# Layer 2's attention in units of one key head, the first batch's run within layer 1's steps and its split weights kept in DRAM for the second

## What is computed

```python
x = layernorm(x + attn(x, Wq, Wk, Wv, Wo))   # layer 1: 16 heads of 128, a token sees 5 blocks of 64
# layer 2, for each batch b:
scores = x[b] @ w_router                     # one score a token
idx = sort(top_k(scores, 128))               # the 128 best tokens, in order
sel = x[b, idx]                              # batch 0's and batch 1's: S = 256 rows
h = rms_norm(sel, ln1_w)
q, kk, v = h @ wq + bq, h @ wk + bk, h @ wv + bv   # 16 query heads, 8 key and value heads
q, kk = rope(q, pos), rope(kk, pos)
att = softmax(causal(q @ kk.T / sqrt(128)))  # causal over all 256 rows: batch 1 also sees batch 0
x1 = sel + (att @ v) @ wo
mlp = (silu(h2 @ w_gate) * (h2 @ w_up)) @ w_down   # h2 = rms_norm(x1, ln2_w)
out = layernorm(x + scatter(x, idx, gate * (x1 + mlp) + (1 - gate) * sel))
```

## Time and profile before

| | |
|---|---|
| median of 3 runs | 1433.35 us (1432.47 to 1434.08) |
| profiled execution, its own time | 1435.52 us |
| its span, first to last instruction | 1433.5 us |
| mean granted TensorE clock | 0.953 |
| busy: PE, DVE, ACT, POOL | 1286.4, 905.2, 606.8, 313.4 us |

### The profile page before, as it was taken

How to read it: one execution, slowest core, us unless ns; L and a number is a source line. 1 busy time by engine, 2 the same in 40 slices (tenths; PEclk the granted TensorE clock), 3 DMA queues, 4 the chain that set the end, 5 groups by cost and what they waited for, 6 DMA issues and landing times.

```text
span 1433.5 us, 19759 instructions
## 1 busy us (share of the span) xinstructions
PE 1286.4 (90%) x7624; PEld 1145.9 (80%) x7624; DVE 905.2 (63%) x2328; ACT 606.8 (42%) x1388; POOL 313.4 (22%) x221
## 2 busy tenths in 40 slices
PE   6999999999999999999999999999998733767795
PEld 5898989889898988877879898989886633666795
DVE  4556565665565565787866556565556787686465
ACT  4444444444444444333434444444444222435352
POOL 2101120202020111231211021111202462252374
PEclk9999999999999999999999999999998876798798
DMA  5100110101010110133101010101100443253262
GB/s 172 35 22 30 31 44 30 45 16 45 15 45 30 45 65 10 64 99 118 45 26 45 15 45 26 34 30 40 40 33 1 161 147 96 77 170 124 75 207 101
DMA packets 70846, 89.61 MB, mean 63 GB/s; under 512 B 3360, under 2 KB 52512, under 8 KB 70752
## 3 DMA queue, kind: packets, MB, share of 16 engines
q1 hardware_dynamic: 70336, 87.04, 18.7%
q0 software_dynamic: 416, 1.31, 0.3%
HBM read 79.43 MB, written 8.91 MB: 62 GB/s over the span
## 4 chain that ended last, share of the span: by engine, by line
PE 67%; DVE 21%; ACT 7%; issue 3%; DMA 1%; POOL 0%; SPq 0%; ACTq 0%; DVEq 0%; POOLq 0%
PE proj L759 33%; PE y L759 10%; PE s L759 9%; PE o L759 8%; DVE arena L1179 8%; ACT arena L1020 4%; PE tp L831 4%; ACT prob L1054 2%; DVE prob L1214 2%; DVE work L1296 2%; DVE work L1388 1%; DVE yacc L1248 1%; ACT prob L1126 1%; DVE bn_out L1261 1%; DVE work L1391 1%
## 5 line engine op out<-in xcount | busy, mean ns | idle before, releaser
L759 PE MATMUL proj<-arena 128*128 128x256 f32 (+1 forms) x3552 | 649.3, 334 | 11.7 <-DVE arena L1179 7.5
L759 PEld LDWEIGHTS proj<-arena 128*128 128x128 f32 x3552 | 547.6, 192 | 74.1 <-DVE arena L1179 9.6
L1509 POOL TENSOR_TENSOR arena<-wraw,arena 128x1024 fp32r<-128x1024 f32 x98 | 242.8, 2487 | 936.0 <-ACT arena L1020 936.0
L1054 ACT ACTIVATE prob<-prob,stat 128x384 f32<-128x384 f32 (+1 forms) x256 | 151.0, 590 | 499.6 <-DVE stat L1214 499.6
L1179 DVE TENSOR_TENSOR arena<-proj,arena 128x512 fp32r<-128x512 f32 (+1 forms) x282 | 159.1, 569 | 314.1 <-ACT arena L1020 312.8
L759 PE MATMUL o<-arena 128*128 128x256 f32 (+1 forms) x1248 | 255.1, 333 | 8.8 <-DVE arena L1179 5.8
L759 PE MATMUL s<-arena 128*128 128x384 f32 (+3 forms) x1008 | 224.4, 340 | 10.8 <-DVE arena L1179 10.8
L759 PE MATMUL y<-arena 128*128 128x512 f32 (+1 forms) x888 | 214.7, 379 | 8.4 <-DVE stat L1419 4.4
L759 PEld LDWEIGHTS s<-arena 128*128 128x128 f32 x1008 | 175.2, 195 | 30.8 <-DVE arena L1179 15.7
L759 PEld LDWEIGHTS o<-arena 128*128 128x128 f32 x1248 | 185.8, 199 | 15.0 <-DVE arena L1179 7.7
L1179 DVE TENSOR_TENSOR arena<-tp,arena 128x384 fp32r<-128x384 f32 (+2 forms) x273 | 142.4, 522 | 83.5 <-ACT arena L1020 83.0
(11 more groups left out here) (136 smaller groups left out, 565.2 us busy)
## 6 DMA issues: line engine op xcount, KB each, us to landing
wraw<-in_L_attn_Wq SPq DMA_DIRECT2D x16, 512.0 KB, 3.3
wraw<-in_L_attn_Wk SPq DMA_DIRECT2D x16, 512.0 KB, 3.3
wraw<-in_L_attn_Wv SPq DMA_DIRECT2D x16, 512.0 KB, 3.3
wraw<-in_L_attn_Wo SPq DMA_DIRECT2D x16, 512.0 KB, 3.7
wraw<-in_L_ffn_wq SPq DMA_DIRECT2D x16, 512.0 KB, 5.1
yacc<-in_L_attn_hidden_states SPq DMA_DIRECT2D x16, 256.0 KB, 3.0
y_dram<-yacc SPq DMA_DIRECT2D x16, 256.0 KB, 3.2
out<-work SPq DMA_DIRECT2D x16, 256.0 KB, 2.1
```

What stands on the lines that cost most here:

```text
L759: ins = e.matmul(out_ap, l[a], r[b], start=first and i == 0 and j == 0, stop=final and i == n - 1 and j == 2, skip_group_check=skip)
L1054: e.activation(prob[s][:, 0:n], prob[s][:, 0:n], ACT.Exp, bias=stat[:, 4 * s + 1:4 * s + 2], scale=-1.0, accum_out=stat[:, 4 * s + 2:4 * s ...
L1509: e.tensor_tensor(lo, wraw[n % RAW_SLOTS][:], hi.bitcast(F32), ALU.subtract).then_inc(*G_.inc("wsplit", n, "lo"))
```

## The change

Layer 2's attention is cut anew. A **unit** is one key head n with its two query heads: `u1` the product of 512 columns (256 of q, 128 of k, 128 of v) with one piece of `wq` (uA) and one of k and v side by side (uB), its bias and v's split; `ur` the rotation; `u2` the transposes of q and k and their split; `u3` the scores, maximum and exponential; `un` the division; `u4` the transposes of the probabilities; `u5` the product with v; `u6` the product with 256 rows of `wo` (uC). Each is one stage of a generator.

- **Batch 0's** eight units run in groups 11 to 14 of layer 1, two a group, started at r = 2 and r = 9. All PSUM of a unit is one bank: `proj1` for the first, `y` for the second. The gather's follow-up (`routed_in(0)`) moves in front of them. Layer 1's output projection moves by a step, to r = 3 to 10.
- The three split pieces of each unit are written to DRAM (1 MB each, hi and lo, `wsave`), and batch 0's k and v too (`ukeep`). **Batch 1's** units read them back (`wback`, `ukback`) and split nothing. Behind step 255 ten slots take such pieces instead of five.
- Room: `O_SLOTS` falls from 3 to 2, and the transposed probabilities lie in a ring of 5 blocks instead of 8; where a tile's blocks wrap, its split is done in two instructions.
- Behind step 255 only layer 1's end, the choice of batch 1's tokens, and then batch 1's eight units stand, one started at each step. The units share one buffer of probabilities, `uprob`.

```diff
-O_SLOTS = 3
+O_SLOTS = 2
...
+PT_BLOCKS = 5
...
+UNIT_GROUPS = range(NG + 3, NG + 7)
...
+        for G in range(NB * NG):
+            b, g = divmod(G, NG)
+            pieces = dict(q=Wq, v=Wv, k=Wk)
+            stream += [((which, b, g), columns(pieces[which], g)) for which in ("qvk" if G > 0 else "qkv")]
+            if G - 1 in UNIT_GROUPS:
+                stream.append(unit_pieces(2 * UNIT_GROUPS.index(G - 1) + 1)[2])
+            if G >= 1:
+                stream.append((("o", *divmod(G - 1, NG)), rows(Wo, (G - 1) % NG)))
+            if G in UNIT_GROUPS:
+                n = 2 * UNIT_GROUPS.index(G)
+                stream += [*unit_pieces(n), *unit_pieces(n + 1)[:2]]
...
+        for n in range(NKV):
+            stream += [((which, 1, n), None) for which in ("uA", "uB", "uC")]
...
+                if is_kept(n):
+                    saved[slot_of[n]].plan(n)
+                    job("wsave", n)
...
+        def unit(b, n, banks):
             bs = n % 2
+            hold(f"work{bs}", ("ubias", b, n), V_, "ur", b, n, "vlo")
+            job("ubias", b, n)
+            yield
+            need("uA", b, n)
+            need("uB", b, n)
...
+            hold(to["u1"], ("u1", b, n), V_, "u1", b, n, "bias")
+            job("u1", b, n)
+            for which in ("uA", "uB"):
+                retire((which, b, n), "u1", b, n, "made")
+            yield
...
+            job("ur", b, n)
+            yield
...
+            job("u2", b, n)
...
+                job("ukeep", n)
+            yield
...
+            hold("uprob", ("u3", b, n), T_, "u4", b, n, "made")
+            job("u3", b, n)
+            if b == 1 and n + 2 < NKV:
+                bring_back(n + 2)
+            yield
+            job("un", b, n)
+            yield
...
+            job("u4", b, n)
+            yield
...
+            job("u5", b, n)
+            yield
+            need("uC", b, n)
...
+            job(kind, b, n)
+            retire(("uC", b, n), kind, b, n, "made")
...
-            if 4 <= r < 12 and 1 <= G and u < END:
-                project_out(G - 1, r - 4)
+            if 3 <= r < 11 and 1 <= G and u < END:
+                project_out(G - 1, r - 3)
...
-            if u == END - 3:
-                running.append(routed_in(0))
...
-            if u - END in FIRST_STEPS:
-                running.append(project2(0, FIRST_STEPS.index(u - END)))
+            if G in UNIT_GROUPS and r in (2, 9):
+                n = 2 * UNIT_GROUPS.index(G) + (r == 9)
+                running.append(unit(0, n, ["proj1" if r == 2 else "y"] * 6))
+            if u == END - 4:
+                add_slots(XT_SLOTS, "qk", NHEADS - 1, "q", 1, "made")
+            if u == END + 3:
+                add_slots([PT_SLOT], "pv", NHEADS - 1, TT - 1, "made")
...
-        for n in range(len(FIRST_STEPS), len(QKV_ORDER)):
-            step(project2(0, n))
         while len(selected) < NB:
-            step(attend2(0, next(pairs)))
-        step(routed_in(1), attend2(0, next(pairs)))
-        step(attend2(0, next(pairs)))
+            step()
+        step(routed_in(1))
...
-        for k in range(17):
...
+        for k in range(NKV):
+            step(unit(1, k, [f"proj{k % 2}", "s0", "s1", "tp", "y", "o0"]))
...
                 elif kind == "o":
                     H, half = key
                     if H >= O_SLOTS:
-                        act.wait_ge(*T_.at("out", (H - O_SLOTS) // HG, TT - 1, "made"))
+                        act.wait_ge(*T_.at("out", (H - O_SLOTS) // HG, 4 * half + 3, "made"))
...
+                    if tenant[n] is not None and is_kept(tenant[n]):
+                        act.wait_ge(*saved[slot_of[n]].at(tenant[n]))
...
+                elif kind == "wsave":
...
+                    sp.wait_ge(*(G_ if split_on[n] == "G" else V_).at("wsplit", n, "lo"))
+                    e.dma_start(w_dram[3 * m + "ABC".index(which[1])].bitcast(F32), whole[slot_of[n]].bitcast(F32)
+                                ).then_inc(saved[slot_of[n]].sem, 16)
...
+                elif kind == "wback":
...
+                    sp.wait_ge(*saved[slot_of[source]].at(source))
+                    e.dma_start(whole[slot_of[n]].bitcast(F32), w_dram[3 * m + "ABC".index(which[1])].bitcast(F32)
+                                ).then_inc(back_loaded[slot_of[n]].sem, 16)
```

More of the change, by code:

```diff
@@ L453, in build @@
         selected = []
-        rope_taken = []
         def choose(b):
@@ L498, in choose @@
             job("find", b)
-            job("gather", b, *rope_taken)
+            job("gather", b)
             selected.append(b)
+            if not tail:
+                yield
+                yield from routed_in(b)
         h_there = []
@@ L559, in attend2 @@
             yield
[L560 to L569 removed]
+            hold(to["u5"], ("u5", b, n), V_, "u5", b, n, "lo")
+            job("u5", b, n)
+            yield
+            need("uC", b, n)
@@ L571, in residual2, with bring_back @@
+            if b == 0 or n == 0:
+                hold(to["u6"], ("u6", b, n), V_, "u6", b, n if b == 0 else NKV - 1, "sum")
+            kind = "u6" if b == 0 or n == NKV - 1 else "u6part"
+            job(kind, b, n)
+            retire(("uC", b, n), kind, b, n, "made")
+        def bring_back(n):
+            for what in ("k", "v"):
+                kv_back[n % 2].plan(n, what)
+            job("ukback", n)
         def residual2(b):
-            hold(f"work{4 + b}", ("res", b), V_, "fin", b, "row")
@@ new lines, in tensor_program @@
+                    ins.then_inc(*T_.inc("u1", b, n, "made"))
+                elif kind == "u2":
+                    b, n = key
+                    dst = bank[bank_of["u2", b, n]]
+                    pe.wait_ge(*freed(bank_of["u2", b, n], "u2", b, n))
+                    pe.wait_ge(*V_.at("ur", b, n, "sum"))
+                    for k in range(3):
+                        ins = e.transpose(dst[:, k * P:(k + 1) * P], work[4 + n % 2][:, k * P:(k + 1) * P], ident[:])
+                    ins.then_inc(*T_.inc("u2", b, n, "made"))
+                elif kind == "u3":
```

610 lines of the change are left out of this document (317 added, 293 removed).

## The result

The changed kernel takes 1505.8 us (median of 4 runs, 1504.1 to 1507.3) against 1432.9 for the kernel before (4 runs, 1431.9 to 1434.1): ratio 1.0508, 95% interval 1.049 to 1.0526, slower by 73 us. Forecast were 1447 us and a range up to 1470. The direction was right and the size was not. The profiled span is 1505.5 us.

A forecast was written before the change was run, and what follows sets the result against it. TensorE was taken to bound layer 1, and waits the 329 us tail behind step 255. Terms 45 + 41 - 8 - 28 - 37 + 1 - 0.5 gave +13.5 on 1433.5: 1447 us, range 1412 to 1470.

The forecast's parts named there:

- A: Layer 1: TensorE's work for batch 0's eight units, 5.6 us each, costs its full duration, +45 us.
- B: Layer 1's unit groups: TensorE waits for weight splits at r = 4 and r = 12, plus clock and VectorE load, +41 us.
- `O_SLOTS` = 2: Layer 1, r = 10: ScalarE waits 1.4 us for the last output tile; put at nothing, 1 us a group if uncovered.
- The ring: Layer 1: extra instructions for wrapping blocks, 0.25 us in 2 steps of 5; nothing, 1 us a group if uncovered.
- C: End of layer 1's steps: the double split of batch 0's first pieces goes, with its waits, -8 us.
- D: Last output projection and layer norm: without project2, 32 us instead of 60.0, -28 us.
- E: Choice of batch 1's tokens: other work standing in its chain goes, 33 us left of 69.7, -37 us.
- F: Batch 1's units: rounds of 10.3 us through the single `uprob` buffer, then shorter ones; 105 us against 104.6, +1.
- G: Residual, MLP and end: same instructions with one addition less, -0.5 us on 94.9 us.
- Rival 1: Splits hidden in layer 1 and VectorE's reordering free: 1402 us, halfway 1422; chance 0.27 with the halfway case.
- Rival 2: Batch 1's units: returning 1 MB weight pieces bind the rounds at 12.5 us, +15, so 1462 us; chance 0.13.
- rival 3: Layer 1: splits wait for 1 MB saves to land, holding up ScalarE's exponentials, +40, so 1487 us; chance 0.08.

The follow-up runs named there:

- experiment 13: Changed kernel with late output-tile copies, two probability buffers, earlier load of batch 0's norm weights, no weight splits for batch 0's units: 1398.4 us, 0.9757 of the kernel before.
- experiment 8: Changed kernel, but batch 0's units use the group's split Wq piece, without own loads, splits and saves: 1453.7 us, 1.0142 of the kernel before.
- Experiment 6: Changed kernel with low parts of all weight pieces on VectorE instead of GpSimd in the groups with units: 1489.8 us, 1.0401 of the kernel before.
- Experiment 1: Kernel before with two output tiles used instead of three and the output projection one step earlier: 1460.8 us, ratio 1.0202.
- experiment 4: Kernel before, three output tiles kept, with only the output projection one step earlier (r = 3 to 10): 1440.6 us, ratio 1.0049.
- experiment 5: Changed kernel with output-tile copies two steps later and the projection back at r = 4 to 11: 1483.0 us, 1.0342 of the kernel before.
- experiment 2: Kernel before with only the ring of five blocks and its split copies, three output tiles kept: 1435.3 us, ratio 1.0026.
- experiments 10 and 11: Changed kernel with late copies, VectorE low parts, second probability buffer, batch 0's rows normed five steps later: 1454.0 us; then norm weights loaded at the gather: 1450.7 us.
- Experiment 9: Changed kernel with a second buffer for the probabilities of batch 1's odd units: 1483.0 us, 1.0333 of the kernel before.
- experiment 7: Changed kernel saving only unit 0's three pieces (3 saves of 1 MB, not 24), reused by all batch 1 units: 1500.6 us, 1.0485 of the kernel before.
- experiment 14: Kernel before with one edit, output-tile halves copied two steps later: 1421.0 us, ratio 0.9926.

## Why the prediction was too low

**A (+45): right.** Two units cost 12.7 us a group in experiment 13 (against a plain group of 65.8) and 11.6 in experiment 8 (79.4 against 67.8); 11.2 were forecast. At 12 us, four groups are 48.

**B (+41): the waits I named were right; the division that GpSimd holds up was left out, and the clock behind the waits was mis-sized.** At r = 4 TensorE waited 2.1 us in group 13 (forecast 2.2), at r = 12 3.7 and 0.6 (forecast 3.8 and 1.9): 26.0 us in four groups, forecast 32. Not in the sum was the division held up by GpSimd: 12.2 us in four groups. I had weighed it in the sentences on the Trainium skill (SBUF — State Buffer, "Who interferes with whom") and left it out. The trace agrees with that page here, also where it says that a VectorE instruction with both inputs in SBUF contends: the low part of v took 2.48 us, while one that reads one input from PSUM (line 1302) took its usual 0.55 in the same 5.04 us. Experiment 6 shows that GpSimd's low parts cause it: without them the wait falls to 3.4 us. And the clock: I took 5 us for all four groups. TensorE was busy 329.7 us in the four groups, and 310.3 with the same work at full clock in experiment 13, so the lower clock cost some 19. The stretches of 7.5 and 3.4 us shown behind the two long waits of a group ran at 0.58 and 0.57. 26 + 12 + 19 + 48 = 105, measured 102.8; the forecast had 86.

**`O_SLOTS` = 2 at nothing: wrong, and in every group.** The text said "ScalarE waits at r = 10 for the last output tile, 1.4 us, with one exponential behind it that TensorE needs a step later: nothing". The wait came as named, 1.25 us. The cover failed: behind the exponential also stands the step's split of k or q, which the scores of r = 12 need, and the row of the projection that would have filled r = 11 had moved to r = 10. "1 us a group if that cover fails" was in the text too, but not in the sum or the range. Experiment 1 gives 29 us for it together with the projection's earlier place, 7 of them for the place (experiment 4); experiment 5 takes 23 back.

**The ring at nothing:** 4 us (experiment 2).

**The rows of batch 0 in group 10:** not in the prediction at all. Group 10 grew by 8.7 us, of which 3.6 come with the two output tiles (73.6 us in experiment 1). For the rest there is the wait of 3.8 us for the norm. It is one of order on VectorE and not of the gather, which fits that later steps didn't cure it (experiments 10 and 11). The mean clock of that group was 0.93.

**C (-8): not seen.** The last 15 steps took 60.6 us instead of 59.6. With nothing else to fill them, each of the last three transposes waited 1.1 to 1.3 us for its division.

**D (-28): -25.4. E (-37): -40.1.** The two chains were forecast at 32 and 33 us and measured 34.6 and 29.6; that their sum came right to 1 us is partly luck.

**F (+1): the mechanism right, the later rounds wrong.** Experiment 9 shows that the single buffer sets the rounds, since without it the seven together fell from 76.4 to 53.3 us. The first u4 came after 28 us (forecast 29), and the first three rounds, forecast at 10.3 us, took 9.8, 11.2 and 12.4. But I had made those behind them shorter, 7 us each, because u1 falls out of them; they took 10.6, 14.4, 9.6 and 8.4. Without u1, TensorE waited for VectorE instead. In the one of 14.4 the rotation's addition and v's low part on VectorE took 2.64 and 2.43 us beside GpSimd's low parts for the MLP. +6.5 in all.

**G (-0.5):** +1.1.

**The rivals.** Rival 1 (splits hidden) is what experiments 8 and 13 build by leaving the splits out: its gain is real, its condition isn't met. Rival 2 (returning weights bind) falls for the changed kernel with experiment 9, where the same weights come back in rounds of 7.6 us on average instead of 10.9, rival 3 (saves block ScalarE) with experiment 7. The 59 us by which the forecast was low are: 17.4 in the groups 1 to 9, where nothing was forecast (experiment 1 has 16 of them); 8.7 in group 10, likewise; 16.8 in the groups with units (102.8 against 86), by the held division and the clock; 9 at the end of the steps (C); and 6.6 behind them. Of the signs named, the waits at r = 4 and r = 12 were there, but not "nowhere else as long": the four for the division lasted 3.0 to 3.1 us. The range failed because the rivals varied B and F only (and the saves), and no case had a price for what stood at nothing.

## What to carry to other kernels

An instruction that is made to wait in front of the critical engine's supplier, once in every group, must be costed by everything queued behind it until the critical engine's next need, in that step's own length; "one exponential behind it" was two instructions in a step that the same change had shortened. An item put at nothing belongs into the range with its price times the number of groups, and a wait of TensorE costs more than itself, since the clock falls behind it: here 38 us of waits in four groups brought 19 more. Where an engine looks full, a copy that nobody needs yet at the front of its supplier's queue can still cost it: the two-step delay of experiment 14 gave 0.7% for a few lines.
